# Adding x inside y's accumulation on TensorE, and moving two kinds of copies to ScalarE, in the opening of an LRU, attention and MoE kernel

## The reference, cut to what matters

```python
x = u                                          # (4, 1024, 128) float32: B = 4 batches of 1024 tokens
n = layernorm(x)
Bu = einsum('blh,nh->bln', n, B_re + 1j*B_im) * gamma
s = associative_scan(Lam, Bu)                  # a linear recurrence along the 1024 tokens, 64 complex states
y = einsum('bln,on->blo', s, C).real + einsum('blh,oh->blo', n, D)
x = x + y                                      # the sum that the change is about
z = layernorm(x)
a = rmsnorm(z) * ln1_w
q, k, v = a @ wq.T, a @ wk.T, a @ wv.T         # 16 heads of 8
h = z + softmax(q k^T / sqrt(8)) v @ wo.T
h = h + moe(rmsnorm(h) * ln2_w)                # 8 experts, two per token
out = x + h
```

## Time and profile before

| | us |
|---|---|
| median of 3 runs | 997.0 (996.48 to 999.84) |
| the profiled execution | 999.88 |
| its span, from first to last instruction | 998.1 |
| PE, DVE, ACT, POOL busy in the span | 872.4, 855.8, 705.4, 389.5 |
| mean granted clock of PE | 0.964 |

### The profile page before, as it was taken

How to read it: one execution, slowest core, us unless ns; L and a number is a source line. 1 busy time by engine, 2 the same in 40 slices (tenths; PEclk the granted TensorE clock), 3 DMA queues, 4 the chain that set the end, 5 groups by cost and what they waited for, 6 DMA issues and landing times.

```text
span 998.1 us, 18349 instructions
## 1 busy us (share of the span) xinstructions
PE 872.4 (87%) x5978; PEld 362.2 (36%) x5978; DVE 855.8 (86%) x1462; ACT 705.4 (71%) x1511; POOL 389.5 (39%) x615
## 2 busy tenths in 40 slices
PE   0578788999999999999999999999999999889980
PEld 0265531222222222222222222222322246688980
DVE  6988888999999998989989998898799966668662
ACT  1765424888888888888888888888788876545650
POOL 7213340011010054434604535363687403336774
PEclk9798896999999999999999999999999999999995
DMA  7997740011000110101101010010101111122445
GB/s 248 388 393 243 217 125 18 10 33 25 10 25 15 28 25 9 46 11 29 51 10 25 15 43 28 14 47 9 25 31 45 26 39 47 46 60 67 113 150 190
DMA packets 60830, 74.34 MB, mean 74 GB/s; under 512 B 9153, under 2 KB 39105, under 8 KB 60353
## 3 DMA queue, kind: packets, MB, share of 16 engines
q1 hardware_dynamic: 55408, 63.40, 20.9%
q0 software_dynamic: 4608, 9.58, 2.8%
q10 hardware_dynamic: 720, 0.20, 0.1%
HBM read 28.09 MB, written 44.79 MB: 73 GB/s over the span
## 4 chain that ended last, share of the span: by engine, by line
PE 57%; DVE 22%; ACT 9%; issue 6%; POOL 4%; DMA 1%; POOLq 0%; ACTq 0%; DVEq 0%; SPq 0%
PE ps L1690 20%; DVE nmax L1242 12%; PE ps L1680 9%; PE ps L1568 8%; ACT prob L994 7%; PE ps L1789 6%; PE ps L1805 3%; PE ps L1750 2%; PE ps L1587 2%; PE ps L1557 2%; POOL by_token L821 2%; PE ps L1713 1%; POOL by_expert_rows L742 1%; DMA xacc<-x 1%; PE ps L1529 1%
## 5 line engine op out<-in xcount | busy, mean ns | idle before, releaser
L1242 DVE TENSOR_REDUCE nmax<-ps 128x1 f32<-128x1024 f32 x512 | 602.1, 1219 | 42.5 <-PE ps L1568 38.0
L994 ACT ACTIVATE prob<-ps 128x512 f32<-128x512 f32 x1024 | 529.6, 603 | 81.6 <-PE ps L1680 80.0
L1568 PE MATMUL ps<-packs 50*128 50x512 bf16 x1024 | 344.0, 390 | 8.9 <-DVE nmax L1242 5.0
L1680 PE MATMUL ps<-packs 50*128 50x512 bf16 x1024 | 313.6, 385 | 30.4 <-ACT prob L994 20.4
L1690 PE MATMUL ps<-prob,vpad 128*32 128x512 f32 x2048 | 273.8, 607 | 0.0
L1568 PEld LDWEIGHTS ps<-packs 50*128 50x128 bf16 x1024 | 74.6, 94 | 232.3 <-DVE nmax L1242 175.5
L1680 PEld LDWEIGHTS ps<-packs 50*128 50x128 bf16 x1024 | 75.9, 94 | 148.8 <-ACT prob L994 95.5
L553 POOL MEMSET packs<- 2x2048 bf16 x32 | 57.5, 1797 | 172.8 <-PE ps L1680 171.6
L821 POOL DMA_INDIRECT by_token<-wk,vall x80 | 79.8, 997 | 97.5 <-DVE wk L1332 61.0
L1789 PE MATMUL ps<-ws 128*128 128x128 f32 x640 | 87.6, 281 | 3.1 <-DVE ws L1352 2.3
L1789 PEld LDWEIGHTS ps<-ws 128*128 128x128 f32 x640 | 79.0, 194 | 9.0 <-issue 7.2
(11 more groups left out here) (307 smaller groups left out, 880.5 us busy)
## 6 DMA issues: line engine op xcount, KB each, us to landing
by_expert_rows<-prob SPq DMA_DIRECT2D x4, 5016.0 KB, 31.9
packs<-k_parts SPq DMA_DIRECT2D x32, 192.0 KB, 3.4
packs<-q_parts SPq DMA_DIRECT2D x64, 96.0 KB, 2.8
vall<-by_expert_rows SPq DMA_DIRECT2D x80, 66.0 KB
packs<-by_token SPq DMA_DIRECT2D x8, 512.0 KB, 4.6
w<-w_t SPq DMA_DIRECT2D x3, 1024.0 KB, 15.5
q_parts<-front SPq DMA_DIRECT2D x16, 192.0 KB, 3.3
k_parts<-front SPq DMA_DIRECT2D x16, 192.0 KB, 3.4
```

The source lines that it names most:

```text
L994: act.activation(prob[:, v % RING, :], bank(col_bank(pos)), ACT.Exp).then_inc(col_free, 1)
L1242: dve.tensor_reduce(nmax[:, half, par, pair, qt:qt + 1], bank(first, 2), AX_X, ALU.max, negate=True).then_inc(row_free, 1)
L1568: ins = pe.matmul(bank(first + kh), qpack[r:r + ROWS, slot, half, pair, qt * P:(qt + 1) * P], kpack[r:r + ROWS, slot, pair, kh * HALF:(kh ...
L1680: pe.matmul(bank(col_bank(pos)), kpack[r:r + ROWS, slot, head // 2, kt * P:(kt + 1) * P], qpack[r:r + ROWS, slot, half, head // 2, :], sta ...
```

## The change

On PE, `product_y(b)` for b of 1 to 3 begins with 8 products of the identity with the tiles of `xacc`; they open the accumulation in banks 6 and 7, ahead of the wait for `z_ready`, and the 24 products of y add onto them. On ACT, `act_batch(b)` for b of 0 to 2 gets two steps between the high parts and `keep_z(b)`: `middle_parts(b)` makes the middle parts of q and k (2 ACTIVATEs of 128x1024), which POOL made before, each waiting for DVE's `rest`; and `save_sums(b + 1)` copies the sums of the next batch out of banks 6 and 7 into `xacc` (2 ACTIVATEs of 128x512), each waiting for `y_done`. DVE's `norm_a` for b of 1 to 3 has no add any more and waits for `sums_saved` instead. POOL makes the middle parts of batch 3 alone. PE's waits on `y_taken` become waits on `sums_saved`, save for batch 0, where all stays as it was.

```diff
@@ -209,7 +209,7 @@
         act_self = sem("act_self")
         lam_ready, sin_ready = sem("lam_ready"), sem("sin_ready")
         trig_red = sem("trig_red")
-        y_taken = sem("y_taken")
+        y_taken, sums_saved = sem("y_taken"), sem("sums_saved")
         bu_read, centred, pool_centred = sem("bu_read"), sem("centred"), sem("pool_centred")
         b_scaled = sem("b_scaled")
         u_turned, bu_done, y_done, a_turned, qk_done, v_done = (
@@ -591,7 +591,8 @@
 
                 for w in range(2):
                     gp.wait_ge(rest_left, 2 * b + w + 3)
-                    gp.tensor_copy(parts[:, w, 1, :], rest[:, w, :]).then_inc(mid_ready, 1)
+                    if b == B - 1:
+                        gp.tensor_copy(parts[:, w, 1, :], rest[:, w, :]).then_inc(mid_ready, 1)
                     gp.wait_ge(mid_ready, 2 * b + w + 1)
                     gp.tensor_tensor(parts[:, w, 2, :], rest[:, w, :], parts[:, w, 1, :],
                                      ALU.subtract).then_inc(lo_ready, 1)
@@ -924,6 +925,19 @@
                             ps[:, first + half, :].rearrange("p (t c) -> p t c", t=4)[:, :, 32 * j:32 * j + 32], ACT.Copy)
                 ins.then_inc(v_saved, 1)
 
+            def middle_parts(b):
+
+                for w in range(2):
+                    act.wait_ge(rest_left, 2 * b + w + 3)
+                    act.activation(parts[:, w, 1, :], rest[:, w, :], ACT.Copy).then_inc(mid_ready, 1)
+
+            def save_sums(b):
+
+                for half in range(2):
+                    act.wait_ge(y_done, 2 * b + half + 1)
+                    act.activation(xacc[:, b * TILES + half * 4:b * TILES + half * 4 + 4, :]
+                                   .rearrange("p t h -> p (t h)"), bank(6 + half), ACT.Copy).then_inc(sums_saved, 1)
+
             def act_batch(b):
                 last = b == B - 1
                 if b + 2 < B:
@@ -940,6 +954,8 @@
                     act.activation(parts[:, w, 0, :], bank(2 if last else 2 + 2 * w, 2), ACT.Copy,
                                    scale=(scale, 1.0)[w]).then_inc(hi_ready, 1)
                 if not last:
+                    middle_parts(b)
+                    save_sums(b + 1)
                     keep_z(b)
                 if b + 3 < B:
                     norm_u(b + 3)
@@ -1193,11 +1209,14 @@
             def norm_a(step, b):
 
                 for half in range(2):
-                    dve.wait_ge(y_done, 2 * b + half + 1)
-                    xb = xacc[:, b * TILES + half * 4:b * TILES + half * 4 + 4, :].rearrange("p t h -> p (t h)")
-                    step(dve.tensor_tensor(xb, bank(6 + half), xb, ALU.add))
-                    if half:
-                        dve.sem_inc(y_taken, 1)
+                    if b == 0:
+                        dve.wait_ge(y_done, half + 1)
+                        xb = xacc[:, half * 4:half * 4 + 4, :].rearrange("p t h -> p (t h)")
+                        step(dve.tensor_tensor(xb, bank(6 + half), xb, ALU.add))
+                        if half:
+                            dve.sem_inc(y_taken, 1)
+                    else:
+                        dve.wait_ge(sums_saved, 2 * (b - 1) + half + 1)
                     for t in range(half * 4, half * 4 + 4):
                         ins = dve.bn_stats(st6[:, t, :], tile(xacc, b, t))
                 step(ins)
@@ -1547,6 +1566,9 @@
 
             def product_y(b):
 
+                for t in range(TILES if b else 0):
+                    pe.matmul(bank(6, 2)[:, t * P:(t + 1) * P], ident[:, :], xacc[:, b * TILES + t, :],
+                              start=(t % 4 == 0), stop=False, skip_group_check=True)
                 for t in range(TILES):
                     if t % 4 == 0:
                         pe.wait_ge(z_ready, b * 4 + t // 2 + 2)
@@ -1554,7 +1576,7 @@
                     o = bank(6, 2)[:, c]
                     for k, (lhs, rhs) in enumerate(((x_cos, wC[:, 0, :]), (x_sin, wC[:, 1, :]), (u_T[b % 2], wD[:, :]))):
 
-                        ins = pe.matmul(o, lhs[:, c], rhs, start=(k == 0 and t % 4 == 0), stop=(k == 2),
+                        ins = pe.matmul(o, lhs[:, c], rhs, start=(not b and k == 0 and t % 4 == 0), stop=(k == 2),
                                         skip_group_check=True)
                     if t % 4 == 3:
                         ins.then_inc(y_done, 1)
@@ -1600,7 +1622,7 @@
                     turn_u(b + 2)
                 product_bu(b + 1)
                 if b:
-                    pe.wait_ge(y_taken, b + 1)
+                    pe.wait_ge(sums_saved, 2 * b)
                     project_v(0, TILES, first=6).then_inc(v_done, 1)
                 if b + 2 < B:
                     pe.wait_ge(uT_saved, b + 3)
@@ -1611,7 +1633,10 @@
                     project_half(w, 2 + 2 * i, 0)
                     project_half(w, 2 + 2 * i, 1).then_inc(qk_done, 1)
                 pe.wait_ge(v_saved, b)
-                pe.wait_ge(y_taken, b + 1)
+                if b:
+                    pe.wait_ge(sums_saved, 2 * b)
+                else:
+                    pe.wait_ge(y_taken, 1)
                 product_y(b + 1)
                 if b == B - 2:
                     project_v(0, TILES).then_inc(v_done, 1)
```

## The result

| | before | after |
|---|---|---|
| median of 5 runs, us | 997.0 (996.48 to 999.84) | 1008.71 (1006.01 to 1009.34) |
| the profiled execution, us | 999.88 | 1008.95 |
| its span, us | 998.1 | 1007.2 |
| mean granted clock of PE | 0.964 | 0.963 |

The changed kernel is slower: ratio 1.0096, 95% interval 1.0080 to 1.0111, which is 9.6 us of 997.0. The two profiled executions stand 9.1 us apart, the medians of the five runs 11.7, their means 10.2.

What follows compares the result with a forecast made beforehand. In the opening it took ACT to bound step 0, then PE, DVE and ACT in turn. Steps of +6.8, +0.5 and +3.3 gave +10.6, the two clock terms cancelling: 1007.7 from the median 997.0, range 1003.2 to 1012.0.

Steps and rivals of the forecast that it cites:

- step 0: Opening, ACT: `keep_z(0)` starts at 76.2 instead of 69.4 behind waits for DVE and PE, +6.8 us.
- 1: `turn_a(2)` against step 0: Step 1, from y of batch 2 to the roots: 1.79 − 0.84 + 0.65 − 1.08, +0.5 us at `turn_a(2)`.
- (a): Before `turn_a(2)`: PE's pause shrinks from 3.0 to 1.7 us; if the clock holds, q and k gain 2.9 us.
- 2: identity products: Step 2, PE: the identity products come after q and k, +1.79 us.
- 2: end of y to first scores: Step 2, ACT: second copy, `keep_z(2)` and `save_v(2)` all follow y of batch 3, 5.3 us instead of 3.31, +2.0.
- (b): Before the last half: PE's pause grows from 1.56 to 3.6 us, two score units and 24 unused products slow, +2.9 us.
- L1215: Small DVE operation in the opening: no longer meets POOL's subtraction, takes 0.17 us everywhere, −1.08 us in step 1.
- rival 1: The clock falls before `turn_a(2)` as before, and before the last half: +13.5 us, 1010.5; chance 0.15.
- rival 2: The clock holds before `turn_a(2)` and before the last half: +7.7 us, 1004.7; chance 0.17.
- Rival 3: DVE's list is what counts, so fewer adds and no stall make the kernel faster: −6.5 us, 990.5; chance 0.04.
- Rival 4: Step 0's delay is taken up later by PE's waits before `turn_a(2)` and in the last half: 997 to 1000; chance 0.05.
- Rival 5: Part of the waiting in line isn't there, for instance since ACT's copies overlap better: +3 to +7 us; chance 0.09.

Runs made afterwards that it cites:

- the two halves: Middle parts alone on ACT, against the kernel before: 1.0020. Sums alone, the changed kernel with middle parts back on POOL: 1.0095.
- the filled kernel before: The kernel before plus products nothing reads in two PE pauses, 28 ahead of `turn_u(3)` and 24 ahead of `turn_a(2)`: 0.9996.
- the filled changed kernel: The changed kernel with unread products in three PE pauses (68 at the head of step 1, 12 ahead of `turn_a(2)`, 24 ahead of first scores): 1.0042.

## Why the prediction was right, point by point

It gave 1007.7, and the median is 1008.7. The mechanism is the one that was forecast; that the number is so close is in part luck. On the profiled executions it gave +10.7 and got +9.1, which is 1.6 off: one term was too large by 1.7, one was missing, and the median of the kernel before lay 2.9 below its profiled execution, that of the changed one 0.2 below.

| step | forecast, us | in the trace | measured |
|---|---|---|---|
| 0: `keep_z(0)` | +6.8 | 69.40 to 75.90 | +6.5 |
| 1: `turn_a(2)` against step 0 | +0.5 | 106.09 to 113.03 | +0.4 |
| (a): q and k of batch 2 | -2.9 | 6.56 to 3.70 | -2.9 |
| 2: identity products | +1.8 | 118.87 to 120.65 | +1.8 |
| 2: end of y to first scores | +2.0 | 3.31 to 5.03 | +1.7 |
| (b): units and 24 products | +2.9 | 3.34 to 4.55 | +1.2 |
| 2: wait before `turn_a(3)` | -0.5 | 0.49 to none | -0.5 |
| sum, at `turn_a(3)` | +10.6 | 127.48 to 135.79 | +8.3 |

- **Step 0 right.** ACT is what `turn_u(3)` waits for, and it waits in line. The experiment on ACT's order shows this (76.97), and the two halves show that the wait for y, not the 3.4 us of copies, decides. The identity products took 1.78 us (68.07 to 69.85; forecast 1.79), a sum 0.58 to 0.60 (0.60), a middle part 1.10 (1.02).
- **But a part of it was put too high.** The prediction put 1.79 of the 6.8 on the identity products. The one clean comparison, with filled pauses, gives them 1.0 us at `keep_z(0)` (75.68 and 74.64): without them ACT's second middle part ends last. The unfilled kernel without x can't tell, since it lost 1.4 us ahead of the edit.
- **L1215 right.** It took 0.17 in both steps where it took 1.46 and 1.25. In step 1 this is worth 1.1 us on the chain (102.16 against 103.29). The Trainium skill (SBUF — State Buffer, section "SBUF: two separate sides") calls the port that DVE and POOL share an exclusive lock, and these runs agree: the small DVE operation is long where it meets POOL's subtraction (118.67 to 120.14, beside 117.98 to 120.11, in the filled kernel before) and 0.17 us where that is over.
- **(a) right, and with luck.** The clock held over 1.75 us. With 1.99 us (x left out), 1.98 (middle parts alone) and 3.0 (before) it fell, and in the kernel with ACT's other order it was at half for q after 1.75 us too. So rival 1 was near.
- **(b) mis-sized.** The direction was right: the clock was 0.50 after 3.28 us of pause. But it was back at full after 134.2, and the piece took 4.55 us, where the prediction left nearly all of it at half (6.2). The row it used, 22 products in 4.67 us, was a piece almost wholly at half clock. The same piece took 4.56 and 4.60 us in two other profiled kernels (ACT's other order, the changed kernel again), but 6.06 and 6.07 in two more (x left out, sums alone), after pauses of 3.27 to 3.33 us. So the term is +1.2 in some executions and +2.7 in others, and no run shows what decides. The Trainium skill (TensorE: Matmul & The Clock Gate, section "HAM oscillation") warns of pauses that throw PE back to half clock, and the trace agrees in kind: 0.50 behind this one.
- **A term missing.** At the mark the loss is 8.25 us. PE runs the scores behind it at half clock until 178.3 (before, until 169.5), and the loss is 9.0 us at the row maxima there (170.19 to 179.15); the rest of the span adds 0.1. The prediction let everything behind `turn_a(3)` shift as a whole.
- **The rivals.** By the number alone rival 2 (+7.7), 1.4 us from the profiled difference, is as near as the forecast, 1.6 from it; rival 1 (+13.5) is 4.4 away. The trace decides, since the clock held at (a) and fell at (b). Rival 3 falls: DVE waited 9.68 us for Bu. Rival 4 falls: nothing took the delay up. Rival 5 falls in step 0, which came within 0.3.
- **POOL and SP.** The prediction gave nothing for the earlier middle and low parts, because the first scores waited for v on ACT. In the changed kernel that is so (131.24). It did not see how near SP's queue and DVE's list are in step 2: it would have taken a faster kernel to meet them, and the filled one did.
- **A count.** The prediction speaks of four DVE adds for each step; it is two, six in all. The sum did not use the four.

What stays open: on the medians the loss is 11.7, in the trace 9.1. The means give 10.2 and the ratio 9.6, and the 17 later runs of the kernel before have a median of 998.96, which would make it 9.8; so 997.0 was probably a low draw, and with it the hit within 1 us. The runs of one kernel lie up to 8.4 us apart in these experiments (1050.49 to 1058.89 for the filled kernel before). A clock that falls in some executions after such a pause and holds in others would do that, but no run isolates it. One execution of the filled changed kernel took 1968.02 us; its ratio leaves this out, and nothing here explains it.

## What to carry to other kernels

An engine with an in-order list pays for moved work by what stands behind it: ask first what the new instruction waits for, and who waits for the instruction behind it. Here 3.4 us of copies cost 6.5, and the share of busy time named the wrong engine to relieve. Where a clock follows pauses, a gain of 2 us can be worth nothing (x left out), so compare orders with filled pauses, and look in both traces whether a new pause has taken the place of the filled ones. When a bound is taken away and nothing comes of it, look at the next engine and the DMA queue on the same stretch, and at the pause that the earlier work leaves behind.

## What the runs showed of the hardware

- **The clock near two microseconds of pause.** Before `turn_a(2)` it held after 1.74, 1.75 and 1.81 us and fell after 1.98, 1.99, 3.0. In the kernel with ACT's other order 1.75 us of pause was followed by q at half (3.68) and k at full (1.88), and without x a pause of 0.67 us behind 12 unread products was followed by q mostly at half (3.40). So the length of the pause alone doesn't decide it; what else does, the runs don't settle.
- **How long it stays at half varies too.** After pauses of 3.27 to 3.33 us, the same 28 bfloat16 products took 4.55, 4.56, 4.60, 6.06 and 6.07 us in five profiled kernels.
- **Filling alone can be worth nothing.** Unread products held the clock through 12 us of Bu, v and a, and through q and k of batch 2, and the whole was 0.9996: the pause that was gone came back before `turn_a(3)` as 3.25 us. The same kind of fill in the changed kernel gave back 4.4 us at the mark.
- **Chips differ.** The kernel before took 998.96, 1053.66 and 1055.58 us on three chips. The changed kernel on the third chip was profiled with PE's waits at L1814, in the experts, at 17.7 us against 3.1, ACT's exponentials waiting 97.0 us against 82.3, and a busy time of PE of 892.4 against 876.5, in the attention and the experts, while its opening ended at 169.71 against 169.35. What makes this isn't known from these runs.
